# A graph layer pair on one core: first layer's table built beside the scan, second layer in columns with four edge buffers

## What is computed

```
h  = relu(layernorm(x))
wh = h @ weight                       # 4 heads of 32
e  = leaky_relu(parent_i + child_j)   # parent, child: wh with the attention vectors
x  = x + softmax_over_neighbours(e) @ wh
h  = relu(layernorm(x))
msg = relu((adj @ h) @ W_msg.T + b_msg)
x  = x + gru_cell(msg, h)             # r, z = sigmoid, n = tanh(i_n + r * h_n), (1-z)*n + z*h
```

## Time and profile before

| | us |
|---|---|
| median of 3 runs (1158.62 to 1164.36) | 1160.13 |
| the profiled execution | 1159.31 |
| its span, first to last instruction | 1157.6 |
| ACT busy | 686.2 |
| PE busy | 679.1 |
| POOL busy | 592.6 |
| DVE busy | 586.4 |
| adj loads: half a tile, issue to landing, median | 14 to 15 |

### The profile page before, as it was taken

One profiled execution on the slowest core, in us unless ns is written; L12 is line 12 of the kernel. 1 busy time (PEld: TensorE's weight loads), 2 busy tenths in 40 slices (PEclk: granted clock), 3 DMA queues, 4 the chain that ended last, 5 costly groups with the idle time before them and its releaser, 6 DMA issues. The chain is left out here.

```text
span 1157.6 us, 14697 instructions
## 1 busy us (share of the span) xinstructions
PE 679.1 (59%) x4141; PEld 523.0 (45%) x4141; DVE 586.4 (51%) x2487; ACT 686.2 (59%) x723; POOL 592.6 (51%) x598
## 2 busy tenths in 40 slices
PE   0076555765665566566566566655332776777774
PEld 0064334554454454354354444444331565555563
DVE  4632524656656646747647647557331244433443
ACT  0497866886887887788778778772210333233331
POOL 0021074464564654654744744735705777777770
PEclk9997887888788788778878878876555989899998
DMA  7748999999999999999999999951101222222220
GB/s 237 308 149 306 428 401 413 412 411 416 393 396 413 390 413 407 389 406 405 393 413 403 392 413 398 388 224 20 42 5 44 60 67 68 57 68 70 67 66 25
DMA packets 58623, 311.92 MB, mean 269 GB/s; under 512 B 15577, under 2 KB 32994, under 8 KB 42210
## 3 DMA queue, kind: packets, MB, share of 16 engines
q1 hardware_dynamic: 30434, 277.37, 58.8%
q0 software_dynamic: 19712, 30.02, 10.7%
q10 hardware_dynamic: 8448, 4.20, 1.2%
HBM read 298.82 MB, written 12.71 MB: 269 GB/s over the span
## 5 line engine op out<-in xcount | busy, mean ns | idle before, releaser
L457 ACT ACTIVATE ind<-adj_in 128x4144 bf16<-128x4144 int32 (+1 forms) x128 | 461.9, 3609 | 39.1 <-DMA adj_in<-in_adj 22.8
L397 POOL DMA_INDIRECT rows_in<-wh_table,idx x192 | 198.2, 1032 | 304.4 <-DVE val_idx L869 250.7
L602 PE MATMUL ps<-ind,bit_w 128*128 128x296 bf16 (+1 forms) x1792 | 312.2, 340 | 0.0
L602 PEld LDWEIGHTS ps<-ind,bit_w 128*128 128x128 bf16 x1792 | 206.9, 115 | 89.9
L1030 POOL DMA_INDIRECT rows_in<-g_table,idx x192 | 197.6, 1029 | 91.3 <-issue 54.0
L401 POOL DMA_INDIRECT vals_in<-in_adj,val_idx x192 | 183.6, 956 | 58.6 <-issue 58.6
L799 DVE MAX8 cand<-ps 128x8 f32<-128x148 f32 x256 | 61.9, 304 | 117.6 <-PE ps L602 117.2
L598 PE MATMUL ps<-idx_r,idx_w 128*128 128x296 bf16 x128 | 44.2, 346 | 129.8 <-ACT ind L457 129.6
L1164 DVE TENSOR_SCALAR ownT<-iota,edge_row 128x128 f32<-128x128 f32 x64 | 14.7, 324 | 152.6 <-DMA rows_in<-g_table,idx 152.5
L598 PEld LDWEIGHTS ps<-idx_r,idx_w 128*128 128x128 bf16 x128 | 15.8, 123 | 140.4 <-ACT ind L457 126.5
L619 PE MATMUL ps<-rest,tri 128*128 128x4 f32 x32 | 9.0, 352 | 115.0 <-DVE rest L833 115.0
(11 more groups left out here) (220 smaller groups left out, 1514.7 us busy)
## 6 DMA issues: line engine op xcount, KB each, us to landing
adj_in<-in_adj SPq DMA_DIRECT2D x64, 2072.0 KB, 15.0
adj_in<-in_adj SPq DMA_DIRECT2D x64, 2024.0 KB, 14.0
wh_table<-t_buf POOLq DMA_DIRECT2D x16, 264.0 KB, 3.0
g_table<-t_buf ACTq DMA_DIRECT2D x16, 256.0 KB, 25.1
out<-adj_in SPq DMA_DIRECT2D x16, 256.0 KB, 2.3
rows_in<-wh_table,idx POOLq DMA_INDIRECT x192, 6.7
vals_in<-in_adj,val_idx POOLq DMA_INDIRECT x192, 6.7
rows_in<-g_table,idx POOLq DMA_INDIRECT x192, 2.8
```

The source lines that it names most:

```text
L397: nc.gpsimd.indirect_dma_start(out=rows_in[:, par, t, k, :], out_offset=None, in_=wh_table, in_offset=bass.IndirectOffsetOnAxis(ap=idx[:, ...
L457: nc.scalar.activation(ind[:, t % 2, a:b], adj_in[:, slot, 0:b - a].bitcast(I32), ACT.Relu, bias=1.0, scale=-1.0, accum_out=empty[:, bass. ...
L602: ins = nc.tensor.matmul(o[:, 0:w], bit_w[:, b, :], ind[:, t % 2, c0:c0 + w], start=False, stop=(b == BITS - 1))
```

## The change

Two parts.

Front: adj loads are the first on SP's queue; x comes in eight DMAs on POOL's queue, weights and attention vectors on ACT's, biases on SP's behind the first four loads (seven of them new, as columns). The variance is made by quarters of x. The group work of the table is woven into the scan of the first two groups (`units(m)` names the groups of half tile m: two each for m = 2 to 7, one each for m = 8 to 11). Normalising moves from ACT to DVE without the relu, which ACT now applies on the transposed columns. project uses banks 5 and 6 alone. pack is split by halves in the whole scan. The bias rows are made at half tile 13.

Second layer: gathers go to `edges_in` (four buffers) straight by `nbr_idx`, 192 written out; edges are PE's stationary operand, so messages come out in columns; biases are added by ACT and DVE per partition; gates are 512 columns wide with sigmoid; the new state is transposed back to rows. The group order is longer: DVE weights group q + 2, then finishes group q.

```diff
+W_DMAS = 4 + 2 * H
+B_DMAS = 9 + 7
+XC = 16
+RING = 4
 TW = D + H
...
+arena2 = ind[:].rearrange("p b c -> p (b c)").bitcast(F32)
+h2T = carve(arena2, 0, 4)
+msgT = carve(arena2, 4, 2)
+h2r = carve(arena2, 6, 2).rearrange("p b (g d) -> p b g d", g=G)
...
+def units(m):
+    if 2 <= m < 2 * G:
+        return (2 * m - 4, 2 * m - 3)
+    if 2 * G <= m < 3 * G:
+        return (m + G,)
+    return ()
+
+def turn_bank(q):
+    return 4 if q % 2 and q < 3 * G else 7
 
...
         def load(tile, half, slot):
             a, b = CUT[half], CUT[half + 1]
             sp.dma_start(adj_in[:, slot, 0:b - a], adj[bass.ds(tile * P, P), a:b]).then_inc(adj_sem[slot], 16)
 
         for n in range(SLOTS):
             load(n // 2, n % 2, n)
+        sp.wait_ge(const_done, 1)
+        for r in (0, 32, 64):
...
+        for c in range(T // XC):
+            for n in range(2):
+                tt = c * XC + n * (XC // 2)
+                pool.dma_start(x1[:, tt:tt + XC // 2, :], x_rows[:, tt:tt + XC // 2, :]).then_inc(x_in[c], 16)
 
...
+        def deviation0(c):
+            act.wait_ge(var_done, c + 1)
+            nc.scalar.activation(sd0[:, c * XC:(c + 1) * XC], var0[:, c * XC:(c + 1) * XC], ACT.Sqrt, bias=epsc[:, 0:1]) \
+                .then_inc(sd_done, 1)
+
+        def turned0(q):
             act.wait_ge(htr_done, q + 1)
-            if not isinstance(q, int) or q >= 2:
+            if q >= 2:
                 act.wait_ge(wh_done, q - 1)
-            nc.scalar.activation(hT[:, par].rearrange("p g d -> p (g d)"), ps[:, (7, 4)[par], :], ACT.Identity,
-                                 accum_out=hsum[:, bass.ds(q, 1)]).then_inc(hT_done, 1)
-
...
+            def scan(t, half):
+                indicate(s, t, half)
+                if isinstance(s, int) and s < 2:
+                    m = s * 2 * G + 2 * t + half
+                    if m < T // XC:
+                        deviation0(m)
+                    for q in units(m):
+                        turned0(q)
+
+            if "c" in do:
...
+        def turn0(q):
             pe.wait_ge(h_done, q + 1)
-            if not isinstance(q, int) or q >= 2:
-                pe.wait_ge(hT_done, q - 1)
-            for t in range(G):
-                ins = nc.tensor.transpose(ps[:, (7, 4)[par], t * P:(t + 1) * P], h_buf[:, par, t, :], ident[:])
+            if q >= 1:
...
+        def project(q):
             pe.wait_ge(hT_done, q + 1)
-            if not isinstance(q, int) or q >= 2:
-                pe.wait_ge(table_rows, q - 1)
-            for t in range(G):
-                ins = nc.tensor.matmul(ps[:, (5, 2)[par] + t // 2, (t % 2) * (TW + H):(t % 2 + 1) * (TW + H)], hT[:, par, t, :], wx[:],
+            if q >= 1:
+                pe.wait_ge(table_rows, q)
+            for t in range(G):
+                ins = nc.tensor.matmul(ps[:, 5 + t // 2, (t % 2) * (TW + H):(t % 2 + 1) * (TW + H)], hT[:, q % 2, t, :], wx[:],
...
+        def mean_row():
+            pe.wait_ge(hbar_done, 1)
+            pe.wait_ge(table_rows, NG)
+            nc.tensor.matmul(ps[:, 5, 0:D], hbar_b[:], wx[:, 0:D], start=True, stop=True).then_inc(whbar_mm, 1)
...
+            for half in range(2):
+                pe.wait_ge(ind_done, tile * 2 + half + 1)
+                if half == 0 and (not isinstance(tile, int) or tile >= 2):
+                    pe.wait_ge(seg_done, tile - 1)
+                for u in range(2):
+                    o = ps[:, (t % 2) * 2 + u, 0:HALF]
+                    if half == 0:
+                        nc.tensor.matmul(o, idx_w[:], idx_r[:, u * HALF:(u + 1) * HALF], start=True, stop=False)
+                    for b in range(half * (BITS // 2), (half + 1) * (BITS // 2)):
+                        c0 = b * WORDS + u * HALF
+                        w = min(HALF, N - c0)
+                        ins = nc.tensor.matmul(o[:, 0:w], bit_w[:, b, :], ind[:, t % 2, c0:c0 + w],
+                                               start=False, stop=(b == BITS - 1))
+                if half:
+                    ins.then_inc(pack_done, 1)
+                if isinstance(s, int) and s < 2:
+                    m = tile * 2 + half
+                    for q in units(m):
+                        project(q)
+                    for q in units(m + 1):
+                        turn0(q)
+                    if m == 3 * G:
+                        mean_row()
...
+        def variance0(c):
+            dve.wait_ge(x_in[c], 32)
+            for t in range(c * XC, (c + 1) * XC):
...
+        def norm0(c):
+            dve.wait_ge(sd_done, c + 1)
+            link(V.reciprocal(columns_of(rs0, c), columns_of(sd0, c)))
+            link(V.scalar_tensor_tensor(out=columns_of(nmr0, c), in0=columns_of(mean0, c), scalar=-0.5, in1=columns_of(rs0, c),
+                                        op0=ALU.mult, op1=ALU.mult))
+
+        def rows0(q):
+            if q >= 2:
+                dve.wait_ge(htr_done, q - 1)
+            for t in range(G):
+                n = q * G + t
+                ins = V.tensor_scalar(h_buf[q % 2][:, t, :], x1[:, n, :], rs0[:, n:n + 1], nmr0[:, n:n + 1], ALU.mult, ALU.add)
+            ins.then_inc(h_done, 1)
+
...
+        def table(q):
+            dve.wait_ge(wh_done, q + 1)
+            if q >= 2:
+                dve.wait_ge(table_out[q % 2], (q // 2) * 16)
...
+        variance0(0)
+        variance0(1)
+        norm0(0)
...
-        restart()
+        rows0(0)
+        rows0(1)
+        variance0(2)
+        norm0(1)
+        variance0(3)
+        norm0(2)
+        norm0(3)
...
+        def woven(m):
+            for q in units(m):
+                table(q)
+            for q in units(m + 1):
+                if q >= 2:
+                    rows0(q)
+            if m == 3 * G - 1:
+                mean_row()
+            if m == 3 * G + 1:
+                bias_rows()
+                dve.wait_ge(whbar_mm, 1)
+                link(V.tensor_copy(whbar[:], ps[:, 5, 0:D]))
...
+            def gather(q):
+                if q >= RING:
+                    pool.wait_ge(agg2_mm, q - RING + 1)
                 for t in range(G):
                     for k in range(3):
                         nc.gpsimd.indirect_dma_start(
-                            out=rows_in[:, par, t, k, 0:D], out_offset=None, in_=g_table,
-                            in_offset=bass.IndirectOffsetOnAxis(ap=idx2[:, par, t, k:k + 1], axis=0),
-                        ).then_inc(gathered2[par], 16)
+                            out=edges_in[:, q % RING, t, k, :], out_offset=None, in_=g_table,
...
-            gather(1, 1)
-            with pool.Fori(1, NG // 2) as i:
-                for par in range(2):
-                    pool.wait_ge(agg2_mm, i * 2 + par - 1)
...
+            def prepare(q, k):
+                par = k % 2
+                if not isinstance(q, int) or q >= 2:
+                    dve.wait_ge(agg2_mm, q - 1)
                 for t in range(G):
                     V.tensor_scalar(ownT[:, par, t, :], iota1[:], edge_row[:, tiles(q * G + t, 1)], None, ALU.is_equal)
-                r = rows_in[:, par].rearrange("p g k c -> p (g k) c")[:, :, 0:D]
+                dve.wait_ge(edges_landed[k], (q - k) * (3 * G * 16 // RING) + 3 * G * 16)
+                r = edges_in[:, k].rearrange("p g k c -> p (g k) c")
                 V.tensor_tensor(r, r, nbr_val[:, tiles(q * G), :].rearrange("p g k -> p (g k)").unsqueeze(2)
                                 .to_broadcast([P, 3 * G, D]), ALU.mult).then_inc(weighted2, 1)
...
+            def candidate(q):
+                dve.wait_ge(rz_done, q * 2 + 1)
+                dve.wait_ge(gate_mm, q * 3 + 3)
+                V.scalar_tensor_tensor(out=uT, in0=ps[:, 3, :], scalar=bias_in[:, 5:6], in1=rT, op0=ALU.add, op1=ALU.mult) \
+                    .then_inc(half_done, 1)
+                dve.wait_ge(half_done, q + 1)
+                V.tensor_tensor(uT, uT, ps[:, 2, :], ALU.add).then_inc(pre_done, 1)
...
+            def add_rows(q, k):
+                par = k % 2
+                dve.wait_ge(rows_mm, q + 1)
                 if not isinstance(q, int) or q >= 2:
                     dve.wait_ge(out_done[par], (q - par) * 8)
-                dve.wait_ge(dve_step, q * 4 + 3)
-                V.scalar_tensor_tensor(out=fin[:, par], in0=rh[:], scalar=0.5, in1=nt[:], op0=ALU.mult, op1=ALU.add) \
+                V.tensor_tensor(fin[:, par], ps[:, 4, :].rearrange("p (g d) -> p g d", g=G), x1[:, tiles(q * G), :], ALU.add) \
...
+            def mix(q, k):
+                dve.wait_ge(n_done, q + 1)
+                V.tensor_tensor(dT, h2T[:, k, :], nT, ALU.subtract).then_inc(diff_done, 1)
+                dve.wait_ge(rz_done, q * 2 + 2)
+                dve.wait_ge(diff_done, q + 1)
+                V.tensor_tensor(dT, dT, zT[:, k % 2, :], ALU.mult).then_inc(mixed_done, 1)
+                dve.wait_ge(mixed_done, q + 1)
+                V.tensor_tensor(newT[:, k % 2, :], dT, nT, ALU.add).then_inc(new_done, 1)
+
+            def body(q, k, before=True, after=True):
```

(63 more changed lines are left out.)

376 lines of the change are left out of this document (152 added, 224 removed).

## The result

The changed kernel takes 1175.42 us (median of 4 runs, 1170.98 to 1176.85) where the kernel before, on the same chip, takes 1159.75. The ratio of the means is 1.0121, 95% interval 1.0082 to 1.016 (ratios with an interval are always of the means, beside runs of the kernel before on the same chip): slower by 1.2%, where 1144 was forecast. The profiled execution took 1174.5 us with a span of 1172.7, so 15.1 us more span than before.

A forecast was written before the change was run, and what follows sets the result against it. Adjacency loads (DMA) were taken to bound the scan, POOL's gather issue layer two. Front -14, scan -2.5, first gather -0.5, layer two 0, tail +1.5 sum to -15.5: 1144 us; range 1123 to 1160, the forecast's own 1135 to 1153.

The forecast's parts named there:

- The front, -14: Start of the kernel: with table work woven into the scan, half tile 16's load lands at 142.4 against 156.06 us.
- x is complete at 50 us: Front: x finishes loading at 50 us, after six or seven adjacency loads have run; bounds 20 and 60.
- the sum's 62.5: Front: half tile 2's step ends at 62.5 us, 12.5 us after x is complete.
- 9.0 us: Front, half tiles 3 to 7: each step with two groups is a serial chain of 9.0 us, five making 45.
- Steps 8 to 10: Front: three one-group steps of 5.76 us make 17.3, plus 1.8 for DVE's search and 3.9 for PE's lists.
- The yardstick: Front: time ACT takes up half tile 16, 156.06 us before; its load was forecast to land at 142.4.
- rival D: Front: table chain at TensorE's lower clock, +20 us over five two-group steps, total time 1170 us; chance 0.09.
- rival C: Front gives nothing: weights or x at 62 us rather than 50, total time 1156 to 1160 us; chance 0.16.
- The scan, -2.5: Scan: the pack starting on a first half shows only after the last load, -2.5 us (bounds -2 to -4).
- First gather, -0.5: Start of layer two: first gather waits for the last store alone, no index copy; -0.5 us (0 to -1.5).
- Layer two, 0: Layer two's gathers: POOL's issuing covers all and never waits for a buffer, so 0 us; bounds -10 to +10.
- Tail, +1.5: After the last gather to the output's issue: 25.5 to 26 us against 24.5, +1.5 (0 to +8).

The follow-up runs named there:

- e_chain: e_after_pad80 with three early adjacency loads held until weights and x land, bias loads behind x, and table steps' rows and transposes reordered: 1130.8 us, ratio 0.9762.
- e_split: The kernel before with only the pack split by halves in the whole scan: 1134.25 us, ratio 0.9791.
- e_after_pad80: The changed kernel with 80 memsets that compute nothing added on DVE ahead of its scan loop, shifting the loop's place: 1147.02 us, ratio 0.9896.

## Why the prediction was wrong

*The front, -14.* It came out at +3.0 by half tile 19. In parts:
- "x is complete at 50 us": wrong, and that the step behind it ends nearly on time is luck. x is complete by 40.4 us: it is loaded by quarters, in turn with the adjacency loads, and is not held back until they are through, as I had argued from the stores' landings. But DVE comes to its rows only at 45.0, behind the attention vectors (41.87) and what is made of them, and to the last two quarters' variance at 47.1 and 51.5. Half tile 4 is taken up at 65.8; the sum's 62.5 for the end of the step and ACT's two groups of 0.8 ahead of it make 64.
- "9.0 us" for a step with two groups: 10.3 (half tile 4 at 65.75 to half tile 9 at 117.43). The four normalising operations of a group take DVE 1.1 us where I had 0.9. The half packs of the five steps take 2.7, 2.9, 3.6, 3.7 and 3.6 us where I had 2.0, together 6.5 more, which is about all of the five steps' +6.7. That the chain is serial was right (e_chain).
- Steps 8 to 10: some 3 us more. Half tile 12 then comes at 142.9 instead of 131.3. Half tile 13 comes 4 us late behind it: ACT waits 4.1 us for PE's lists (recv), a wait that the sum doesn't have.
- The yardstick itself: I had load 16 land at 142.4 and stopped there. Half tiles 13 to 15 stand before it on ACT at 3.65 us each, so even on my numbers it could not be taken up before 146. In the changed kernel they run 3.6 apart from 150.79 to 161.55, with the loads long there.

The half packs bear on rival D, the table chain at TensorE's lower clock. The mean from 0 to 152 us (0.92 before, 0.88 after) hides it; here are the steps of the changed kernel, and then the table stage of the kernel before, which I had held against this rival (the columns are those of the earlier trace rows; the granted clock is 0.81 and 1.00):

```profile
60.00:130.00 70.00, 44.90 (x253) 33.82 (x251) 30.59 (x120) 33.48 (x38) 9.62 (x13) 0.81 0.73 251
```

```profile
60.00:90.00 30.00, 22.22 (x163) 18.91 (x162) 11.46 (x39) 29.08 (x80) 9.26 (x12) 1.00 0.40 131
```

So D named a true cause, the clock of the chain, and priced it three times too high: at most some 6.5 us over five steps, where it had 20. With the fetches taken away the front is worth +6 against e_split (half tile 127 at 763.0 against 757.4), so by its size rival C, "the front gives nothing", came nearest; its cause, weights or x at 62 us, did not occur.

*The scan, -2.5.* This is the step that failed most, and twice, in opposite directions: the sum has nothing for it but the pack after the last load, and the scan measured +8.3. I wrote that "DMA engines are full (1.00)" and that ACT follows them, so the split pack could gain only at the end. Alone it gains 24 us (e_split): 1.3 us in each of 13 groups and the rest at the ends. A DMA share of 1.00 at 402 GB/s was not a ceiling: 414 GB/s show the same share, and ACT's waits for loads, 3.4 us in 48 half tiles, said that it did not follow them. The repetition of 44.37 us, group after group, fits that: a cycle of engines. Then what comes with the place of DVE's loop, of which the sum has nothing, takes 28 us back.

*First gather, -0.5, and the emptying.* Together with the split's 2.5 that makes -3.0; measured -2.7. Right.

*Layer two, 0.* Measured +4.7 for the gathers, inside the bounds of 10 either way. "POOL never waits for a buffer" was right, so four buffers could give nothing, and the row of the one long gather gave the right mechanism. The size failed: I counted five operations with two SBUF inputs against four and hoped for the phase. What counts is which of them begin while a gather is open: one mix operation did before, two do now.

*Tail, +1.5.* Measured +1.8. Right.

Summed again from measured parts: split -24.4, front +5.6, layer two +7.1 give 1160 - 11.7 = 1148, and 1147.0 is measured for e_after_pad80; with the 28 us of the loop's place, 1175. The first and the third part were measured alone; the other two are differences of e_after_pad80 itself, so the sum adds up by their making.

*Open.* That the place of DVE's loop costs the 28 us is shown by moving it, in both directions; how it costs them is not. DVE's late start explains some 2 us of the 6.4 in every two groups. The rest shows as a lower DMA rate at a full share, which no run took apart. That 65 instructions precede the counted ones is only inferred, and so is the rule of three blocks, from seven starts. No run shows what made the slow chip slow.

## What to carry to other kernels

A long loop has a place in its engine's program, and code added far ahead of it can push it over a boundary: compare the instruction queues of the two profiles and look for "issue" idle ahead of a loop's first operation before explaining a slower rate. Then ask when the data of that operation were ready: only what comes after that is the stall's. A full DMA share is not a bound by itself; look how long the engine behind the loads waits for them, and the cheapest test is to release one wait. A mean clock over a whole stage can hide the stretch that matters. While POOL issues gathers, give DVE operations with one SBUF tensor or a PSUM operand, made ahead of the landing; together with a shorter table chain that made a version of 1112.8 us, 3.9% under the kernel before.

## What the runs showed of the hardware that was not expected

- One and the same DVE loop of 314 instructions runs with or without instruction packets on each pass (5 of 8 KB) by where it begins, and a run of some 1147 us becomes one of 1175. With packets DVE starts the pass's first operation 1.8 to 2.2 us after its data are ready (the changed kernel), without them 0.03 us (e_after_pad80). At 517, 5 beyond a multiple of 128, it stays; at 774, 6 beyond one, it doesn't (on the slow chip).
- The DMA engines show a share of 1.00 at 388, 402 and 414 GB/s (400 to 760 us in the changed kernel, the kernel before and e_after_pad80).
- The issue of one column load of 0.5 KB held SP's queue for 6.2 us. The twelve small bias loads issued ahead of it, from 3.0 to 7.6 us, took 0.25 to 0.66 us each, though adjacency loads were under way then too, so what makes an issue long isn't isolated.
- A gather that meets a DVE operation with two SBUF inputs ends 0.82 us after it, whether that lasts 1.76 or 0.69 us.
